# Two row-adding stores under way at once in the expert stage of a decoder layer, with the count to wait for read from a table

## The reference

```
logits = flat_x @ W_router + b_router              # 4096 rows, 8 experts
top_vals, top_idx = top_k(logits, 2)
router_weights = softmax over the two chosen
for e in range(8):
    h = relu(flat_x @ W1[e] + b1[e])               # 256 -> 1024
    y = h @ W2[e] + b2[e]                          # 1024 -> 256
    final_output += y * router_weights[:, e] * (e was chosen)
x = x + final_output
```

## Time and profile before

| | before |
|---|---|
| time, median of 3 runs (range) | 1683.29 us (1679.12 to 1683.64) |
| the profiled execution's own time | 1683.91 us |
| its span in the profile | 1682.1 us |
| busy: PE, DVE, ACT, POOL | 94%, 70%, 55%, 23% |
| share of the chain that ended last: PE, DMA | 69%, 20% |

### The profile page before, as it was taken

How to read it: one execution, slowest core, us unless ns; L and a number is a source line. 1 busy time by engine, 2 the same in 40 slices (tenths; PEclk the granted TensorE clock), 3 DMA queues, 4 the chain that set the end, 5 groups by cost and what they waited for, 6 DMA issues and landing times.

```text
span 1682.1 us, 30734 instructions
## 1 busy us (share of the span) xinstructions
PE 1587.9 (94%) x10398; PEld 959.8 (57%) x10398; DVE 1176.0 (70%) x2413; ACT 931.7 (55%) x1776; POOL 379.2 (23%) x451
## 2 busy tenths in 40 slices
PE   5899999999999999999999999989999988988895
PEld 2423334344454444444434443469999988988895
DVE  4788887888777778777788776433544767767774
ACT  2136656666546667655676657842222656665662
POOL 6200120002200041210031100331342333433333
PEclk9779999999999999999999999999999999999998
DMA  6821540233140440323422613335667555655563
GB/s 173 156 70 33 97 80 13 31 42 58 48 79 26 73 81 8 42 57 86 67 52 43 141 34 118 115 122 153 176 196 217 157 165 161 185 163 175 170 180 82
DMA packets 92668, 173.37 MB, mean 103 GB/s; under 512 B 13235, under 2 KB 51123, under 8 KB 92384
## 3 DMA queue, kind: packets, MB, share of 16 engines
q1 hardware_dynamic: 75376, 143.69, 34.1%
q0 software_dynamic: 15744, 26.54, 7.4%
q10 hardware_dynamic: 1392, 1.18, 0.3%
HBM read 133.69 MB, written 37.29 MB: 102 GB/s over the span
## 4 chain that ended last, share of the span: by engine, by line
PE 69%; DMA 20%; issue 3%; DVE 3%; ACT 3%; POOL 1%; ACTq 0%; POOLq 0%; SPq 0%; DVEq 0%
DMA out<-yo,xi 19%; PE ps L1102 15%; PE ps L1128 14%; PE ps L1088 13%; PE ps L1294 5%; PE ps L1320 5%; PE ps L1158 3%; PE ps L1180 2%; PE ps L1149 2%; PE ps L1214 2%; DVE rmax L1508 2%; PE ps L1091 2%; PE ps L1131 2%; ACT prob L1338 1%; PE ps L1167 1%
## 5 line engine op out<-in xcount | busy, mean ns | idle before, releaser
L1508 DVE TENSOR_REDUCE rmax<-ps 128x1 f32<-128x512 f32 x1024 | 665.0, 686 | 204.0 <-PE ps L1128 104.3
L1338 ACT ACTIVATE prob<-ps 128x512 f32<-128x512 f32 x1024 | 559.8, 601 | 332.2 <-PE ps L1091 182.7
L1128 PE MATMUL ps<-stacked_k,stacked_q 112*128 112x512 bf16 x1024 | 396.3, 391 | 12.4 <-DVE rmax L1508 6.6
L1088 PE MATMUL ps<-stacked_q,stacked_k 115*128 115x512 bf16 x1024 | 358.7, 382 | 4.8 <-ACT prob L1338 3.2
L1294 PE MATMUL ps<-xiT,w_now 128*128 128x128 f32 x2272 | 270.5, 277 | 30.4 <-issue 30.2
L1294 PEld LDWEIGHTS ps<-xiT,w_now 128*128 128x128 f32 x2272 | 262.8, 193 | 37.2 <-issue 36.1
L1102 PE MATMUL ps<-prob,values 128*32 128x512 f32 x2048 | 273.6, 606 | 5.3 <-ACT prob L1338 5.3
L1128 PEld LDWEIGHTS ps<-stacked_k,stacked_q 112*128 112x128 bf16 x1024 | 100.5, 99 | 288.5 <-DVE rmax L1508 203.5
L1886 POOL DMA_INDIRECT out<-yo,xi x71 | 128.4, 1808 | 347.0 <-DMA out<-yo,xi 233.9
L1088 PEld LDWEIGHTS ps<-stacked_q,stacked_k 115*128 115x128 bf16 x1024 | 98.3, 98 | 159.7 <-ACT prob L1338 78.5
L1444 ACT ACTIVATE hidT<-ps,b 128x128 f32<-128x128 f32 x284 | 81.0, 367 | 126.9 <-PE ps L1294 126.6
(11 more groups left out here) (194 smaller groups left out, 1806.9 us busy)
## 6 DMA issues: line engine op xcount, KB each, us to landing
w_now<-in_w SPq DMA_DIRECT2D x71, 1024.0 KB, 5.4
stacked_q<-parts_of_rows SPq DMA_DIRECT2D x90, 128.0 KB, 6.9
stacked_k<-parts_of_rows SPq DMA_DIRECT2D x90, 128.0 KB, 7.1
xi<-expert_rows SPq DMA_DIRECT2D x71, 130.0 KB, 2.1
w<-in_w SPq DMA_DIRECT2D x8, 1024.0 KB, 9.8
parts_of_rows<-q_part SPq DMA_DIRECT2D x21, 256.0 KB, 8.5
parts_of_rows<-k_part SPq DMA_DIRECT2D x21, 256.0 KB, 8.6
xr<-in_x POOLq DMA_DIRECT2D x4, 1024.0 KB, 8.9
```

The source lines that it names most:

```text
L1088: m = e.matmul(ps[:, bank, :], ka[i][0:ROWS, hh, kt * P:(kt + 1) * P], qa[i][0:ROWS, hh, ch * BANK:(ch + 1) * BANK], start=True, stop=True)
L1128: m = e.matmul(ps[:, bank, :], qa[i][0:MAX_ROW, hh, qt * P:(qt + 1) * P], ka[i][0:MAX_ROW, hh, kc * BANK:(kc + 1) * BANK], start=True, sto ...
L1338: e.activation(prob[:, u % NPROB, :], ps[:, score_bank(u), :], ACT.Exp).then_inc(sem["exp"], 1)
L1508: e.tensor_reduce(rmax[:, G % 2, hh * NT + qt, kc:kc + 1], ps[:, p.bank("max", *k), :], AX.X, ALU.max).then_inc(sem["maxed"], 1)
```

## The change

The one semaphore `added` becomes two, for stores of even and odd blocks; `landed(e, n)` waits on the one of n's parity until store n has landed. The waits of `load` and `yo` keep their meaning. Store n, from n = 24 on, waits for store n-2 only (the last one for n-1). Whether the store before it must have landed as well is decided by data: the second table step makes one more row of numbers, `landed_of`. It holds for each block the count of the semaphore of the other parity that has to be reached: that of store n-1 where the block's first row doesn't follow the previous block's by 128 (the expert or the region changes) or the block is idle, else that of store n-3. POOL reads it into a register in `yo_weight` n+1, ahead of `added` n, and the last of the three operations of that step (L1478) waits for the count.

```
-                 "context_in", "max_rows", "stored", "scattered", "idle_zeroed", "weights_in", "added",
+                 "context_in", "max_rows", "stored", "scattered", "idle_zeroed", "weights_in", "added0", "added1",
...
+            landed_of = sb("landed_of", [P, NBLK], I32)
...
+        def landed(e, n):
+            e.wait_ge(sem[f"added{n % 2}"], 16 * (n // 2 + 1))
...
                     if n >= NX:
-                        e.wait_ge(sem["added"], 16 * (n - NX + 1))
+                        landed(e, n - NX)
...
-        def weigh(e, n, then):
+        def weigh(e, n, then, fronts=None):
...
+            if fronts:
+                e.wait_ge(*fronts)
             return e.tensor_tensor(w[:, :], w[:, :], x[:, SECOND:SECOND + 1], ALU.add)
...
+                        else:
+                            alone, idle = more_than[:, 1:NBLK], past[:, 1:NBLK]
+                            then(e.tensor_tensor(alone, row_of[:, 1:NBLK], row_of[:, 0:NBLK - 1], ALU.subtract))
+                            then(e.tensor_scalar(alone, alone, float(P), 16.0, ALU.not_equal, ALU.mult))
+                            then(e.tensor_scalar(idle, row_of[:, 1:NBLK], float(NE * REGION), 16.0, ALU.is_ge, ALU.mult))
+                            then(e.tensor_tensor(alone, alone, idle, ALU.max))
+                            for odd in range(2):
+                                blocks = slice(2 - odd, NBLK, 2)
+                                then(e.tensor_scalar(past[:, blocks], steps[:, blocks], 1.0 / 16, -8.0 * (2 - odd), ALU.mult, ALU.add))
+                                then(e.tensor_tensor(landed_of[:, blocks], past[:, blocks], more_than[:, blocks], ALU.add))
...
                     if n >= NY:
-                        e.wait_ge(sem["added"], 16 * (n - NY + 1))
+                        landed(e, n - NY)
...
-                    weigh(e, n, then).then_inc(sem["yo_weight"], 1)
+                    fronts = None
+                    if n > FINE:
+                        if n == FINE + 1:
+                            e.wait_ge(sem["table"], p.upto("table", 1, TABLE_PARTS - 1))
+                        fronts = sem[f"added{n % 2}"], e.value_load(landed_of[0:1, n - 1:n], min_val=16, max_val=16 * NBLK)
+                    weigh(e, n, then, fronts).then_inc(sem["yo_weight"], 1)
...
-                    if n >= 1:
-                        e.wait_ge(sem["added"], 16 * n)
+                    if n >= FINE:
+                        landed(e, n - (1 if n == NBLK - 1 else 2))
+                    elif n >= 1:
+                        landed(e, n - 1)
...
-            e.wait_ge(sem["added"], 16 * NBLK)
+            landed(e, NBLK - 2)
+            landed(e, NBLK - 1)
```

More of the change, by code:

```diff
@@ L1883, in _ @@
                     e.wait_ge(sem["yo"], n + 1)
-                    if n >= 1:
-                        e.wait_ge(sem["added"], 16 * n)
+                    if n >= FINE:
+                        landed(e, n - (1 if n == NBLK - 1 else 2))
+                    elif n >= 1:
+                        landed(e, n - 1)
                     e.indirect_dma_start(t["out"], bass.IndirectOffsetOnAxis(ap=xi[n % NX][:, TOKEN:TOKEN + 1].bitcast(I32), axis=0),
-                                         yo[n % NY][:, :], None, compute_op=ALU.add).then_inc(sem["added"], 16)
-            e.wait_ge(sem["added"], 16 * NBLK)
+                                         yo[n % NY][:, :], None, compute_op=ALU.add).then_inc(sem[f"added{n % 2}"], 16)
+            landed(e, NBLK - 2)
+            landed(e, NBLK - 1)
 def constants():
```

## The result

| | before | after |
|---|---|---|
| time, median (range), 4 runs each | 1681.20 us (1678.48 to 1683.64) | 1636.17 us (1635.28 to 1637.70) |
| ratio to before, 95% interval | | 0.9733 (0.9713 to 0.9754) |
| the profiled execution's own time, and its span | 1683.91 us, 1682.1 us | 1636.82 us, 1635.0 us |

The change made the kernel 2.7% faster, 45 us. The forecast was 1641.0 us, its range 1634 to 1660 us. In the changed kernel L1300 is the old L1294 (first layer), L1063 the old L1057 (second layer), L1288 the old L1282, L1486 the old L1478, L1804 the old L1784 and L1916 the old L1886.

The account below looks back on a forecast made before the run. The prediction took stores that follow one another, 7.75 us each, to bound the kernel, with PE's 6.66 us per block next. Gains of 44.6 and 1.3 us less 3 make 42.9 us, from 1683.9 to 1641.0 us, range 1634 to 1660.

Parts of the forecast that it names:

- The pace: Blocks 26 to 70: stores stop binding and PE sets 6.66 us per block, 293.2 us instead of 337.8, gain 44.6 us.
- The lone stores: Stores that still wait for the one before: 12 before block 69 at a quarter microsecond each, 3 us, bounds 0 and 16.
- the slack: Loop of store, load and first layer: weights ready 17.9 us after `up` n+2, due after 20.0 us, leaving 2.1 us.
- The table step: Eight small DVE operations, at most 2.3 us, delaying `hidT` by 1.3 us under PE's second layer: cost 0, uncovered 1.3 us.
- The register load: On POOL, 46 times between two stores, some 0.5 us each with checks: cost 0, uncovered at most 23 us.
- The end: From the start of `up` 70 to the last store's issue: 13.2 us instead of 14.5, gain 1.3 us.
- The sum: Whole kernel: 44.6 + 1.3 - 3 = 42.9 us gained from the profiled 1683.9 us, giving 1641.0 us.
- the load that takes over: Rival: crowded landings and weight loads use up the slack, 1654 us, or 1665 with another 0.5 us per block; chance 0.13.
- The queue that serializes: Rival: the second store is only worked on when the first has landed, pace 6.8 to 6.9 us, 1651 us; chance 0.07.
- No overlap: Rival: every store is alone or two take twice as long, pace stays 7.7 us, 1684 us; chance 0.05.
- slower: Rival: the loop store, load, `up` of three blocks exceeds 23.0 us, pace 8.3 us, 1711 us; chance 0.05.
- its remark on store 39: Its weights went out 1.43 us later, not 1.1, and the next store followed after 5.21 us, not 7.75.

Follow-up runs that it names:

- c0: The changed kernel run once more with no further edit, on the same chip as three other runs: 1638.21 us, 0.9731 of the kernel before.
- a4: The changed kernel, where from block 29 on a load waits for the landing of store n-4 instead of n-5: 1683.17 us, 1.0006 of the kernel before.
- a1: The changed kernel, where every store from block 24 on waits again for the store just before it: 1684.86 us, 1.0023 of the kernel before.
- b3: The kernel before, loading only 64 of 1024 columns of the first-layer weights from block 28 on: 1641.54 us, 0.9761 of the kernel before.
- b1: The kernel before with one idle register load on SP between xi and the weights from block 28 on: 1642.07 us, 0.9761 of the kernel before.

## Why the prediction was right

*The pace* was right in its cause and nearly so in size: 44.6 us booked, 337.8 - 291.8 = 46.0 us measured. PE's block is 6.63 us, not the 6.66 us of the three blocks that I read in before. Two readings beside it were loose. The waits of PE in the earlier trace rows are those for the weights; the same view has six more for xi, 3.0 us, so the weights were not the only thing that PE waited for. And these waits together, 31.7 us, are less than the 46 us: the forecast came from the distance of the first layers, which holds all of it, and rightly not from the sum of the waits.

*The lone stores* were overpriced. 3 us were booked for 12 of them; PE has no wait at all in `after` and one of 0.3 us in c0. Six of the twelve (24, 33, 40, 50, 53, 59) came 7.4 us or more after the store before, six did not. The working behind it was right: a lone store is about 1.3 us late (these six by 0.8 to 2.0 us), and the slack, 2.1 us in the text and 2.5 us in the median as read under a4, takes it up. By that working the cost was 0; the quarter of a microsecond each was a reserve that no row asked for. It was not far from being needed, as block 64 shows. The landings did get shorter: counted as in the sum, with the 0.7 us, their median is 6.8 us against 7.6, and 18 of 40 are 6.5 us or less, where the text had said half or more. The weights go out 1.25 us (median) behind the nearest store, not the 2.0 us of the text.

*The table step*: eight operations in 1.9 us, 2.3 us booked. The two rows, against the earlier trace rows:

```profile
1273.26 0.20 DVE L1759 TENSOR_TENSOR landed_of<-past,more_than 128x35 int32<-128x35 f32 x1
1274.93 1.13 DVE L1773 TENSOR_SCALAR hidT<-ps,b 128x128 f32<-128x128 f32 x4 [1.48 <-issue]
```

`hidT` came 2.0 us later than before, 1.3 us booked, and PE did not wait: the second layer covered it, and a1 shows no cost in all.

*The register load* was as on SP (ns, minimum, median, maximum), and hidden:

```profile
L1899 POOLq TENSOR_LOAD <-landed_of x46: 284/290/508, 1315.2 to 1614.3; - x46
```

*The end*: 14.5 us from `up` 70 to the last store became 1624.16 - 1610.61 = 13.55 us, a gain of 1.0 us, 1.3 booked.

*The sum*: 46.0 + 1.0 and 0.3 us that block 26 started sooner give 47.3 us; between the profiled executions it is 1683.91 - 1636.82 = 47.1 us. The forecast of 1641.0 us was worked out from the profiled execution, so it is to be held against 1636.82 us: of these 4.2 us, 3 are the lone stores and 1.4 the pace.

*The rivals*: the load that takes over is out (no waits of PE; a4 had to take a block away to bring it back). One of its two prices was added up wrongly: another 0.5 us per block is 22 us over 44 blocks, so 1654 us would have become 1676, not 1665; the forecast and its range don't rest on it. The queue that serializes is out at its price: stores are 6.6 us apart, not 6.8 or more, and the landings of stores 33 and 34 were 2.3 us apart, not 6.8. Nor is a store held until the one before it has landed: the first packet of store 41 moved at 1437.58 us, 2.2 us after its issue as in b3, and store 40 landed at 1437.84 us (its load goes out at 1438.57 us). The packets of store 40 had just ended, at 1437.50 us; whether those of two stores would share the engines the changed kernel doesn't show, since there no store was issued so early that they were due together. What overlapped in these pairs was not the moving of data. No overlap and slower are out by the result.

What the prediction did not see is how much lay in its remark on store 39. It used it to say that landings would not get longer. The runs show that it was a remedy by itself: b1 has nearly the whole gain with no two stores under way at once. The slow stores were not slow by nature but had their packets moved behind a megabyte, in nearly every block, because one landing released both the next store and that megabyte. In the changed kernel most stores are released by `yo` instead, which parts the two. How much of its gain is the parting and how much the overlap in 10 of 40 stores was not measured apart. In this respect the size of the gain was not luck: PE's own pace is the floor by either way, and that is what the forecast was made of.

## What to carry to other kernels

Before a second transfer is put under way, look at why the first takes so long: where one event releases a small urgent transfer and a large one that is not urgent, holding the large one back by half a microsecond may give what the overlap gives. A row of transfers that wait for one another gets no shorter by more buffers, so compare its pace with the pace of the bounding engine in a stretch where it runs free; that one comparison gave the gain here to within 2 us. Read the slack of a loop block by block in the kernel itself, as the time from the last issue to the use: taking a block of the loop away shows that the loop is there, but its terms change with it, and the slack came out 2 us too large.

## What the runs showed of the hardware

- A store of 128 rows of 1 KB that adds to HBM lands in 3.8 us (median) with 64 KB of weights beside it (b3), in 5.2 us in b1, where the 1 MB of weights is issued 1.6 us behind half of the stores and sooner behind the rest, and in 6.9 us with the weights issued 1.1 us behind nearly all of them (before). The packets show the order: in the slow case (store 38) none of the store's 144 packets moved in the 5.4 us after its issue, while 386 others with 1.12 MB did. Why a store with its weights 1.4 or 1.6 us behind it is at times quick and at times slow no run shows.
- The first packet of such a store came 2.2 us after its issue when nothing large was ahead of it (the median of 40 stores in b3).
- GpSimd's small operation L1476 that took 3.16 us beside VectorE's work in the earlier trace rows was no exception: its successor in the changed kernel took 2.98 us behind store 33, from 1385.21 us, while `w_low` and `hid_low` ran on VectorE from 1385.23 to 1388.13 us. It cost nothing here, because the store behind it was not yet due.
